# Top-k values of a hybrid block made once a batch and fetched by DMA, roundings of the next projections on GpSimd, and a re-timed order

## What is computed

```
x = x + attention(ln(x))     # 16 heads of 8, softmax over all 1024 keys
x = x + ffn(ln(x))           # 128 -> 512 -> 512 -> 128, weights of +1 and -1
x = x + attn_b(ln(x))        # 8 heads of 16, windows of 64, the nearest 32
x = x + ffn(ln(x))
```

```
q = relu(x @ enc_q);  v = relu(x @ enc_value)
metric = softplus(base + 0.1 * mod(mean of q))
dist[t, j] = sqrt(sum_d (q[j] - q[t])**2 * metric + 1e-8)   # j in t-63 .. t
the 32 nearest j of each t
infl = exp(-dist) / sum
out = (q * (sum_j infl[j] * v[j] + gate * 0.1 * (q / |q|) @ U @ V)) @ decoder
```

## Time and profile before

| | |
|---|---|
| median of three runs | 3110.93 us (3107.17 to 3118.0) |
| the profiled execution | 3113.11 us |
| its span, first to last instruction | 3111.4 us |
| mean granted TensorE clock | 0.907 |
| TensorE busy | 2513.3 us (81%) |
| VectorE busy | 2152.0 us (69%) |
| ScalarE busy | 2328.1 us (75%) |
| GpSimd busy | 645.4 us (21%) |

### The profile page before, as it was taken

The page is one execution under the profiler, slowest core; times in us unless marked ns, Lnnn a source line. Parts: engine busy times, 40 slices in busy tenths (PEclk is TensorE's granted clock), DMA queues, the critical chain, the costliest instruction groups (busy, mean ns, idle before and its releaser), DMA issues.

```text
span 3111.4 us, 71098 instructions
## 1 busy us (share of the span) xinstructions
PE 2513.3 (81%) x21555; PEld 1153.9 (37%) x21555; DVE 2152.0 (69%) x10282; ACT 2328.1 (75%) x3241; POOL 645.4 (21%) x820
## 2 busy tenths in 40 slices
PE   4788788888788887888878887888878888887666
PEld 1112343344333443334433343334433344333454
DVE  5801778856786768956689467875679667982695
ACT  4798669967698677976689676995779877895433
POOL 3010114111241113301142012411124111311331
PEclk6599689999899998999999998998989999999888
DMA  2011001100011000100001000110001000000000
GB/s 87 25 45 39 2 9 40 34 18 6 9 47 34 12 13 11 51 28 9 9 33 38 18 9 9 40 34 19 12 2 60 27 8 2 9 2 1 1 8 8
DMA packets 60961, 67.50 MB, mean 22 GB/s; under 512 B 15602, under 2 KB 41908, under 8 KB 60580
## 3 DMA queue, kind: packets, MB, share of 16 engines
q1 hardware_dynamic: 60336, 62.29, 6.2%
q10 hardware_dynamic: 244, 0.49, 0.1%
HBM read 41.95 MB, written 20.71 MB: 20 GB/s over the span
## 4 chain that ended last, share of the span: by engine, by line
PE 38%; ACT 26%; issue 18%; DVE 11%; POOL 4%; SPq 2%; ACTq 0%; DVEq 0%; DMA 0%; POOLq 0%
PE banks L779 36%; ACT PT L1123 12%; DVE pq L1243 3%; POOL Aop L758 3%; ACT pq L1110 2%; PE banks L786 2%; ACT h L1135 2%; DVE xn L1460 1%; DVE h L1463 1%; ACT hparts L1134 1%; ACT Bs L1034 1%; ACT h L1034 1%; ACT xn L1066 1%; ACT h L1182 1%; DVE stat L1215 1%
## 5 line engine op out<-in xcount | busy, mean ns | idle before, releaser
L1123 ACT ACTIVATE PT<-banks 128x1024 f32<-128x1024 f32 x1024 | 999.9, 1035 | 85.2 <-PE banks L779 77.7
L1243 DVE CUSTOM_DVE_ANT_0 pq<-pq,banks 128x512 f32<-128x512 f32 x1024 | 656.7, 685 | 210.9 <-ACT pq L1110 164.5
L1110 ACT ACTIVATE pq<-banks 128x1024 f32<-128x1024 f32 x512 | 522.8, 1022 | 276.0 <-PE banks L779 252.6
L779 PE MATMUL banks<-PT,Vg 128*9 128x512 f32 x4096 | 550.4, 610 | 2.1 <-ACT PT L1123 2.1
L779 PE MATMUL banks<-Q,K 51*128 51x512 bf16 x2048 | 396.9, 394 | 175.8 <-ACT PT L1123 137.5
L779 PE MATMUL banks<-K,Q 48*128 48x512 bf16 x2048 | 376.3, 440 | 114.1 <-ACT pq L1110 63.9
L742 POOL TENSOR_TENSOR hparts<-h,hparts 128x512 fp32r<-128x512 f32 x112 | 140.2, 1272 | 1099.1 <-ACT h L1135 1099.0
L1460 DVE MATCH_REPLACE8 xn<-h,xn 128x96 f32<-128x96 f32 x1536 | 352.4, 243 | 0.0
L779 PE MATMUL banks<-hparts,W 128*128 128x512 f32 x1024 | 314.5, 437 | 37.1 <-ACT h L1135 30.8
L779 PEld LDWEIGHTS banks<-Q,K 51*128 51x128 bf16 x2048 | 109.5, 93 | 616.3 <-issue 584.6
L1463 DVE MAX8 h<-xn 128x8 f32<-128x96 f32 x1536 | 263.4, 244 | 0.3 <-issue 0.2
(11 more groups left out here) (204 smaller groups left out, 3423.7 us busy)
## 6 DMA issues: line engine op xcount, KB each, us to landing
scratch_k<-pq SPq DMA_DIRECT2D x24, 384.0 KB, 3.1
K<-scratch_k SPq DMA_DIRECT2D x126, 72.0 KB
qkf<-in_hidden_states SPq DMA_DIRECT2D x16, 512.0 KB, 4.4
scratch_q<-pq SPq DMA_DIRECT2D x24, 256.0 KB, 2.5
Q<-scratch_q SPq DMA_DIRECT2D x126, 48.0 KB
K<-scratch_k SPq DMA_DIRECT2D x126, 48.0 KB
Q<-scratch_q SPq DMA_DIRECT2D x126, 32.0 KB
out<-xr SPq DMA_DIRECT2D x14, 256.0 KB, 2.3
```

Of the source, the lines that this page charges most:

```text
L779: return pe.matmul(o, l, r, start=start, stop=stop)
L1110: act.activation(cut(g), ring_pair if work is TURN0 and g % 2 else pair[0], ACT.Relu).then_inc(diff_out.sem, 1)
L1123: act.activation(PT[:, at:at + 2, :], pair[g % ESLOTS], ACT.Exp, scale=1.0 if i % 8 < 4 else -1.0).then_inc(probs.sem, 1)
L1243: dve.tensor_tensor_reduce(r, r, pair[1 + g % 2][:, par, :], 1.0, -3.0e38, ALU.subtract, ALU.max, mred[:, par, i, qt:qt + 1]).then_inc(max ...
```

## The change

**Values.** The stage `vw` is gone. A new stage `ev`, once a batch in the slot of `hid`, multiplies all 1024 reversed tokens by `ev` in eight products in two banks; ScalarE evicts them with a relu into `vrow`, a view of `Bs`; GpSimd sets a column of ones there; SP writes the rows to `scratch_v` and, in a second DMA, repeats the last row 64 times behind them. A new stage `vload`, at the start of each group's slots, brings the group's four windows from there to `Vw`. `keys` waits for both writes before it uses `Bs`, and `pv` for the loads.

**Roundings.** In all batches but the one of the head, the six roundings of the next projections are made by GpSimd itself (`leading`, and stage `split`), each right before its own subtraction. The first `aop` work behind them is as before.

**Paces.** `WEIGHTS`, `TAIL_SPANS` have new numbers. In the list of the loop's second phase most stages keep their place; `wt`/`pv` stand up to one step later and `qk` ahead of the first `wt`. In the first phase some ffn stages move by one `max` step.

```diff
 USES = dict(qk=4, v=2, turn=1, back=1, wo=1, mturn=1, lnT=1, lnTa=2, fa=1, fb=1, fc=1, flip=1, he=1, qd=1, hid=1, mod=1,
-            key=1, pad=1, an=1, qtok=1, hebb=1, dist=2, vw=1, wt=2, pv=1, st=1, dec=1)
+            key=1, pad=1, an=1, qtok=1, hebb=1, dist=2, ev=2, wt=2, pv=1, st=1, dec=1)
...
-WEIGHTS = dict(O=(1.00, 0.33, 1.92, 1.58, 0.47, 1.50, 0.85, 0.85, 1.47, 2.53),
...
-T=(2.57, 2.00, 2.66, 2.50, 2.00, 3.99, 1.50, 1.08,
...
+WEIGHTS = dict(O=(1.00, 0.53, 1.92, 1.58, 0.47, 1.50, 0.85, 0.85, 1.64, 2.40),
...
+T=(2.57, 2.00, 2.66, 2.77, 1.46, 3.81, 1.25, 1.08,
...
 SLOTS_P += norm_slots((1, 1))
-SLOTS_P += [(1, [("flip", 0), ("flip", 1)]), (2, [("he", 0), ("he", 1)]), (2, [("qd", 0), ("qd", 1)]), (1, [("hid", 0)]),
+SLOTS_P += [(1, [("flip", 0), ("flip", 1)]), (2, [("he", 0), ("he", 1)]), (2, [("qd", 0), ("qd", 1)]), (1, [("hid", 0), ("ev", 0)]),
...
     SLOTS_T += [(w, [(stage, n) for real, stage, n in stages if real]) for w, stages in (
-        (3.0, [(_u >= 2, "decd", _u - 2), (_next, "aop", _u + 1), (_last, "vw", _u - 1), (_here, "top", (_u, 0))]),
+        (3.0, [(_u >= 2, "decd", _u - 2), (_next, "aop", _u + 1), (_here, "vload", _u), (_here, "top", (_u, 0))]),
...
 HEAD += [("h", "load", 0), ("h", "tables", 0)] + [("h", "load", n) for n in range(1, NQUAD)]
-TAIL_SPANS = dict(o=(0.000, 0.090), p=(0.075, 0.380), t=(0.380, 1.000), q=(0.380, 0.700), z=(0.723, 0.915))
+TAIL_SPANS = dict(o=(0.000, 0.039), p=(0.034, 0.342), t=(0.380, 1.000), q=(0.380, 0.673), z=(0.723, 0.909))
...
         scratch_k = nc.dram_tensor("scratch_k", [PARTS, P, KT], BF16, kind="Internal").ap()
+        scratch_v = nc.dram_tensor("scratch_v", [RPAD, SH * (SE + 1)], F32, kind="Internal").ap()
...
         m8 = h2[:, 3, P:P + 8 * SH].rearrange("p (h e) -> p h e", e=8)
+        vrow = Bs[:, :].rearrange("p (j h e) -> p j h e", j=NU, e=SE + 1)
...
         gn_l = count("gate_ln", 1)
+        v_ones = count("value_ones", 1)
+        v_out = count("values_out", 2, 16)
+        v_in = [count(f"values_in{i}", NU // 2, 16 * NBLK) for i in range(2)]
...
                             sp.dma_start(Q[r:r + PARTS, n, :, :], m_t[:, par]).then_inc(m_in.sem, 16)
+                    if stage == "ev":
+                        for i in range(2):
+                            sp.wait_ge(*R.moved(c, k + i))
+                            pass_waits(sp)
+                        sp.wait_ge(*v_ones.at(b, 1))
+                        pass_waits(sp)
+                        for i in range(2):
+                            sp.wait_ge(*v_in[i].at(b, 0))
+                            pass_waits(sp)
+                        sp.dma_start(scratch_v[0:T].rearrange("(j p) x -> p j x", p=P),
+                                     vrow.rearrange("p j h e -> p j (h e)")).then_inc(v_out.sem, 16)
+                        sp.dma_start(scratch_v[T:RPAD].unsqueeze(0),
+                                     vrow[P - 1:P, NU - 1].rearrange("p h e -> p (h e)").unsqueeze(1).broadcast_to([1, WIN, SH * (SE + 1)])
+                                     ).then_inc(v_out.sem, 16)
+                    if stage == "vload":
+                        if n == 0:
+                            sp.wait_ge(*v_out.at(b, 2))
+                            pass_waits(sp)
+                        if n >= 2:
+                            sp.wait_ge(*R.filled(c, use["pv", n - 2]))
+                            pass_waits(sp)
+                        for i in range(NBLK):
+                            sp.dma_start(Vw[:, n % 2, i, :, :].rearrange("p h e -> p (h e)"),
+                                         scratch_v[window(NBLK * n + i)]).then_inc(v_in[n % 2].sem, 16)
...
             link(pool.memset(Vg[:, :, :, HD:HD + 1], 1.0))
-            link(pool.memset(Vw[:, :, :, :, SE:SE + 1], 1.0))
...
+            def leading(b, w, work):
+                if w >= 1:
+                    pool.wait_ge(*kd_a.at(b, 1))
+                if work is not FIRST:
+                    pass_waits(pool)
+                    pool.tensor_copy(parts_of(w, 0), whole(w)).then_inc(act_a.sem, 1)
+                pool.wait_ge(*act_a.at(b, w + 1))
+                pool.tensor_tensor(whole(w), whole(w), parts_of(w, 0), ALU.subtract).then_inc(pool_a.sem, 1)
...
-                        pool.wait_ge(*R.moved(c, use["qk", 0] + 2))
-                        pool.wait_ge(*R.moved(c, use["qk", 0] + 3))
+                        for i in range(4):
+                            pool.wait_ge(*R.moved(c, k + i))
                         pool.tensor_tensor(kd, qkf[:, 1, 0:HALF], qkf[:, 1, HALF:T], ALU.add).then_inc(kd_a.sem, 1)
+                        if work is not FIRST:
+                            for part in range(PARTS):
+                                pool.wait_ge(*split_out[part].at(b, 0))
                         for w in range(2):
-                            pool.wait_ge(*act_a.at(b, w + 1))
-                            if w == 1:
-                                pool.wait_ge(*kd_a.at(b, 1))
-                            pool.tensor_tensor(qkf[:, w, :], qkf[:, w, :], parts_of(w, 0), ALU.subtract).then_inc(pool_a.sem, 1)
+                            leading(b, w, work)
                     if (stage, n) == ("split", 0):
-                        pool.wait_ge(*act_a.at(b, 3))
-                        pool.tensor_tensor(kd, kd, parts_of(2, 0), ALU.subtract).then_inc(pool_a.sem, 1)
+                        leading(b, 2, work)
...
                         w = n - 1
+                        if work is not FIRST:
+                            pool.wait_ge(*pool_a.at(b, w + 1))
+                            pass_waits(pool)
+                            pool.tensor_copy(parts_of(w, 1), whole(w)).then_inc(act_a.sem, 1)
...
                         pool.tensor_tensor(sq[:, :], qh[:, :], qh[:, :], ALU.mult).then_inc(sq_p.sem, 1)
+                    if stage == "ev":
+                        pool.wait_ge(*R.filled(c, k))
+                        pass_waits(pool)
+                        pool.memset(vrow[:, :, :, SE:SE + 1], 1.0).then_inc(v_ones.sem, 1)
...
                                               for j in range(4) for i in range(NBLK)])
-                    if stage == "vw":
-                        one(c, k, [(R.bank(k)[0:WW, P * i:P * i + P], xrev[:, window(NBLK * n + i)], ev[:, :], True, True)
-                                      for i in range(NBLK)])
+                    if stage == "ev":
+                        for i in range(2):
+                            one(c, k + i, [(R.bank(k + i)[:, P * q:P * q + P], xrev[:, P * (4 * i + q):P * (4 * i + q) + P], ev[:, :], True, True)
+                                           for q in range(4)])
...
                     if stage == "pv":
-                        pe.wait_ge(*R.made(c, k, use["vw", n], use["wt", n], use["wt", n] + 1))
+                        pe.wait_ge(*R.made(c, k, use["wt", n], use["wt", n] + 1))
+                        pe.wait_ge(*v_in[n % 2].at(b, n // 2 + 1))
+                        pass_waits(pe)
...
                             act.wait_ge(*R.moved(c, k + 2 * w + 1))
-                            if w == 0:
-                                for part in range(PARTS):
-                                    act.wait_ge(*split_out[part].at(b, 0))
-                            act.activation(parts_of(w, 0), qkf[:, w, :], ACT.Identity).then_inc(act_a.sem, 1)
-                    if (stage, n) == ("split", 0):
+                            if work is FIRST:
+                                act.activation(parts_of(w, 0), qkf[:, w, :], ACT.Identity).then_inc(act_a.sem, 1)
+                    if (stage, n) == ("split", 0) and work is FIRST:
...
                         act.activation(parts_of(2, 0), kd, ACT.Identity).then_inc(act_a.sem, 1)
-                    if stage == "split" and 1 <= n <= 3:
+                    if stage == "split" and 1 <= n <= 3 and work is FIRST:
...
                             act.activation(e, e, ACT.Exp, scale=-1.0).then_inc(e_act.sem, 1)
-                    if stage == "vw":
-                        evict(c, k, Vw[:, n % 2, :, :, 0:SE],
-                              R.bank(k)[0:WW, :].rearrange("p (w h e) -> p w h e", w=NBLK, h=SH), ACT.Relu)
+                    if stage == "ev":
+                        for i in range(2):
+                            evict(c, k + i, vrow[:, 4 * i:4 * i + 4, :, 0:SE],
+                                  R.bank(k + i)[:, :].rearrange("p (j h e) -> p j h e", j=4, h=SH), ACT.Relu)
...
                         dve.wait_ge(*R.moved(c, use["pad", 0]))
+                        dve.wait_ge(*v_out.at(b, 2))
```

2 lines of the change are left out of this document (1 added, 1 removed).

## The result

The changed kernel takes 3023.26 us, median of four runs (3018.88 to 3027.61), beside 3112.65 us for the kernel before on the same chip (four runs): a ratio of 0.9713, with a 95% interval of 0.969 to 0.9736. The profiled execution takes 3025.04 us with a span of 3023.3.

What follows compares the result with a forecast made beforehand. ScalarE's work was taken to bound the second phase. The terms, -63.6 + 15 - 7 + 10.5 + 0 + 1 = -44.1, took the profiled 3113.1 us to 3069.0, or 3067 us for the median; range 3036 to 3100.

Steps and rivals of the forecast that it cites:

- Term 1: Second phases: ScalarE loses 10.3 us of evictions and roundings, worth 9.1 us in each of six; in all -63.6 us.
- term 2: Second phases: roundings lengthen GpSimd's queue, so TensorE waits 3.2 us for group 3's operand, not 0.83; +15 over six.
- ScalarE's 0.88: Last batch's second phase: 12.1 us less ScalarE work gave 10.7 us less time, taken as the slope for relief.
- Term 3: Seam of the phases: group 1's product one score pair later fills ScalarE's gap; -1.0 us in seven phases, -7.
- Term 4: First phases: eight values' products and two evictions add 1.5 us in each of seven, +10.5; bounds 0 and +3.5 each.
- Term 5: The values' DMAs: writes hidden behind 16.7 us of maxima before VectorE's key scaling, loads issued early; cost 0.
- Rival D: Values' write lands late, VectorE waits at key scaling: whole gain gone at 19 us, 3161 at 25 us; chance 0.07.
- Term 6: Tail: eight new products +2.2, thirty-two old ones gone 0 to -4, taken as +1; remaining shifts of the paces 0.
- Its own signs: Second phases some 168 us, ScalarE busy 156.5; wrong if its idle grows over 4 us or first phases move over 3.
- Rival B: More comes back: relief one to one, roundings at the memset's price, better paces in half the phases: 3044; chance 0.11.
- Rival A: Gain mostly eaten: roundings dear as subtractions, values' products at upper bound, no seam gain: 3099 or about 3090; chance 0.14.
- C: GpSimd's instructions block VectorE, whose weights reach TensorE late: six phases lose 43 us, giving 3110; chance 0.08.

Runs made afterwards that it cites:

- parts_old_paces: The changed kernel with the old WEIGHTS and TAIL_SPANS: 3080.69 us, ratio 0.9896 to the kernel before.
- distances_later: The kernel before with the distances of group 1 one pair of scores later in the second phase: 3116.83 us, ratio 1.0017.
- values_old_paces: The kernel before with the values made once a batch and fetched by DMA, roundings on ScalarE, old paces: 3106.85 us, ratio 0.9969.
- second_operand_sooner: The changed kernel with third_rounding_later's edit and the operand of group 1 made ahead of the first group's mask: 3016.68 us, ratio 0.9672 to the kernel before.
- third_rounding_later: The changed kernel with the third rounding and its subtraction behind the operand of group 3 on GpSimd: 3003.24 us, ratio 0.9632 to the kernel before.
- values_after_keys: The changed kernel with the values' products moved to the gate's slot, behind the key scaling: 3022.72 us, ratio 0.9718 to the kernel before.

## Why the prediction was right or wrong

- **What bounds the kernel: half right.** ScalarE is the busiest engine of the second phase, and its relief counts most, but the phase is bound by it and TensorE together. "TensorE doesn't step in as the bound" was wrong: TensorE was part of the bound already.
- **Term 1 (relief, -63.6) and term 2 (GpSimd, +15): the sum about right, the split not.** Together -48.6 was forecast in the second phases; parts_old_paces has -53.9. ScalarE's 0.88 is near what the last batch shows for ScalarE alone (0.85). What was missing is TensorE's 8.9 us, costed at nothing: 0.52 to one in the last batch. The last batch lost 9.7 us (8.2 with the old paces) where -4.2 stood; the first, which has the roundings alone, lost 5.2 (4.9) where -4.8 stood. For the roundings alone the forecast's own numbers give about -34 + 15 = -19; measured is -4.2 without the values gone and -25.1 with them. That the sum of the two terms came near is partly luck.
- **Term 2 in detail.** The casts measured 1.04 to 1.07 and 0.61 us for an estimate of 1.4 and 0.8, nearer to the memset than to the subtraction. The queue did not grow (13.7 us for 13.6): the 2.79 us that GpSimd waited for ScalarE had room for them. The wait came out at 2.4 us where 3.2 was forecast; with the old paces, an order that the forecast did not reckon with, it is 3.3. It rose by 1.55 us because TensorE came sooner, and the lowered clock behind it, which was not in the term, added 1.3: 2.8 us a phase for a forecast of 2.5, near by two errors that cancel.
- **Term 3 (-7): the wait went, the time stayed.** distances_later shows 1.6 us less wait in seven batches and no gain.
- **Term 4 (+10.5): right.** First phases of parts_old_paces are +13.0 in sum, 1.9 each for 1.5; in values_old_paces, with the roundings on ScalarE, +17.8, 2.5 each and inside the bounds.
- **Term 5 (0): right.** 3.5 us to landing of a write, 2.1 of a load; 4.2 of the repeated rows; no wait of VectorE. Rival D did not come.
- **Term 6, the tail (+1): not contradicted,** 0.2 us in the kernel after and 2.2 with the old paces, but the tail differs by 5 us between kernels with the same order there.
- **The failed step** is the last sentence of term 6: "The remaining shifts of the paces, one slot here and there: 0, bounds -1 and +1 us in each of 14 phases." Alone they gave -44 us, 3 us a phase, three times the bound. The bound had no row behind it. What the runs show in its place: moving ffn stages by a step took steps 8 to 24 from between 33.8 and 36.5 us to between 32.3 and 32.6, by a better fit at the same clock and by full clock in batches that had 0.95.
- **Its own signs.** The second phases (166.8 us, ScalarE 157.5) and ScalarE's idle time (9.3 us for 8.5) came as foretold. "The first phases move by more than 3 us" was named as a sign of being wrong, and five of seven did, by -5.3 to +3.6 us.
- **Rival B** had the direction (3044) and named the order as a reason, with 7 us for it. Rival A's dear casts and C's blocked VectorE did not come; the blocking that C names is seen at single places (second_operand_sooner), but it did not cost 43 us.

**Still open.** Why the o and q weights fit better was followed to the stretch, not to the one stage. The p weights, behind which 16 us of first phases may stand, and the tail's spans were not tried alone. Why the roundings give 25.1 us when the values are gone, although the wait is then 3.3 us, is not explained. Why a gain of a single move is lost by steps 28 to 44 was not settled, nor was third_rounding_later combined with values_after_keys.

## What to carry to other kernels

When an order written out by hand interleaves several engines, a retimed order is a change of its own: cost it by its own run, or give it bounds as wide as the idle time of the bounding engines, not one slot's worth. Read the slope "time for work" from stretches that differ in one engine's work only; a stretch that lacks work on two engines mixes them, and a wait elsewhere in the stretch can take part of the price back. And where the most loaded engine waits for a small operand, look at the instructions behind the wait as well: moving 1.8 us of foreign work out of the way of that operand gave 3.2 us a phase here.

## What the runs showed of the hardware that was not expected

- One wait of TensorE of 2.3 to 3.4 us was followed by a lower granted clock (0.50 and 0.71 in the 4 us behind it, where it was looked at closely in the kernel after): the 64 matmuls behind it took longer than 1.53 us in 34 of 36 cases, behind waits of 1.6 to 1.9 us at the same place in 4 of 14, and behind waits of 0.5 to 0.9 us in none of 54.
- At the seam of the phases, where TensorE has just waited 3.2 to 4.3 us for the last maxima, the same 64 matmuls take 2.79 us even when their operand is there (second_operand_sooner).
- The same stretch of the same kernel runs at different granted clocks in different batches (0.93 and 0.85), 1.5 us apart, though the instructions are the same.
- GpSimd rounds 1024 columns of float32 to bfloat16 in 1.04 to 1.07 us on average, half of the 2.14 us of a subtraction of the same size.
- A VectorE instruction on 32 columns takes 0.18 us with GpSimd idle, 0.33 us beside GpSimd's Aop, and took 1.40 to 2.18 us behind a GpSimd addition that had started first.
